# An attention block with a mixture of experts on one core: rows of a round fetched by an indirect DMA in place of gather products

## The reference

```python
router_logits = x @ gate_w                                   # x normed, 256 x 512; 64 experts
routing_weights, selected = jax.lax.top_k(router_logits, 8)
routing_weights = jax.nn.softmax(routing_weights, axis=-1)
...
gate = jax.lax.ragged_dot(hidden_sorted, gate_proj_w, group_sizes)    # 512 -> 192 of each token's experts
up = jax.lax.ragged_dot(hidden_sorted, up_proj_w, group_sizes)
down = jax.lax.ragged_dot(jax.nn.silu(gate) * up, down_proj_w, group_sizes)   # 192 -> 512
...
out = jnp.sum(out * routing_weights[..., None], axis=1)
```

## Time and profile before

| what | us |
|---|---|
| median of 3 runs (lowest, highest) | 346.9 (346.42, 350.45) |
| the profiled execution | 346.79 |
| its span, first to last instruction | 345.1 |

### The profile page before, as it was taken

The page is one execution under the profiler, slowest core; times in us unless marked ns, Lnnn a source line. Parts: engine busy times, 40 slices in busy tenths (PEclk is TensorE's granted clock), DMA queues, the critical chain, the costliest instruction groups (busy, mean ns, idle before and its releaser), DMA issues.

```text
span 345.1 us, 8928 instructions
## 1 busy us (share of the span) xinstructions
PE 319.0 (92%) x3096; PEld 179.7 (52%) x3097; DVE 169.4 (49%) x505; ACT 86.4 (25%) x169; POOL 50.9 (15%) x113
## 2 busy tenths in 40 slices
PE   0599999998999978999999999999999999999994
...
PEclk9999999998599999999999999999999999999998
...
GB/s 66 309 394 392 390 355 228 324 1 3 0 2 2 0 0 163 384 4 295 397 392 392 170 0 315 397 379 162 395 391 178 368 393 392 391 391 391 382 17 62
DMA packets 39755, 83.38 MB, mean 242 GB/s; under 512 B 4648, under 2 KB 12976, under 8 KB 39600
## 3 DMA queue, kind: packets, MB, share of 16 engines
...
q10 hardware_dynamic: 416, 0.04, 0.1%
...
## 4 chain that ended last, share of the span: by engine, by line
PE 80%; DVE 9%; ACT 4%; issue 3%; POOL 1%; DVEq 1%; POOLq 0%; ACTq 0%
PE psum L1219 17%; PE psum L1244 15%; PE psum L1181 12%; PE psum L1156 8%; PE psum L974 4%; PE psum L1013 4%; PE psum L986 4%; PE psum L1228 2%; PE psum L1074 2%; PE psum L1232 2%; PE psum L1104 2%; PE psum L965 2%; ACT store L870 1%; PE psum L1058 1%; PE psum L1128 1%
## 5 line engine op out<-in xcount | busy, mean ns | idle before, releaser
L1219 PE MATMUL psum<-store 128*32 128x384 f32 x896 | 77.4, 486 | 0.7 <-ACT store L912 0.7
L1244 PE MATMUL psum<-store 128*32 128x256 f32 (+1 forms) x672 | 54.0, 454 | 0.0
L1181 PEld LDWEIGHTS psum<-store 128*128 128x128 bf16 x696 | 39.5, 97 | 19.7 <-DVE store L771 11.3
L1219 PEld LDWEIGHTS psum<-store 128*32 128x32 f32 x896 | 28.9, 110 | 37.7 <-issue 32.3
L1181 PE MATMUL psum<-store 128*128 128x128 bf16 x696 | 44.5, 219 | 0.9 <-DVE store L771 0.3
L543 POOL TENSOR_TENSOR store<-store 128x256 f32<-128x256 bf16 x28 | 17.2, 613 | 152.7 <-PE psum L1228 152.2
L933 ACT ACTIVATE y_parts<-psum,w_slot 128x512 fp32r<-128x512 f32 x28 | 19.2, 687 | 74.6 <-PE psum L1244 74.6
L1244 PEld LDWEIGHTS psum<-store 128*32 128x32 f32 x672 | 19.0, 109 | 31.7 <-issue 26.9
L1156 PE MATMUL psum<-y_parts,place_T 128*128 128x512 f32 x116 | 34.3, 416 | 0.9 <-ACT y_parts L933 0.9
L799 DVE TENSOR_SCALAR place_T<-psum 128x256 fp32r<-128x256 f32 x28 | 11.9, 424 | 47.0 <-PE psum L1244 47.0
L912 ACT ACTIVATE store<-psum 128x512 f32<-128x512 f32 x29 | 17.3, 598 | 33.8 <-PE psum L1181 33.8
...
## 6 DMA issues: line engine op xcount, KB each, us to landing
store<-n_L_ffn_gate_proj_w_dram SPq DMA_DIRECT2D x64, 384.0 KB, 6.7
store<-in_L_ffn_up_proj_w_dram SPq DMA_DIRECT2D x64, 384.0 KB, 7.0
store<-n_L_ffn_down_proj_w_dram SPq DMA_DIRECT2D x64, 256.0 KB, 7.2
...
```

Of the source, the lines that this page charges most:

```text
L1181: last = pe.matmul(bank[3][:, c * P:(c + 1) * P], xparts[:, h, part, c, :], chosen_slots[:, h], start=(k == 0), stop=(k == 3 * TH - 1))
L1219: last = pe.matmul(bank[0][quarter, 0:2 * INTER], xs[:, c, quarter], w[:, :, c, :], start=(c == 0), stop=(c == DC - 1))
L1244: last = pe.matmul(bank[6][quarter, cols], hidT[:, k, quarter], ring[r][:, e, at:at + cols.stop - cols.start], start=(k == 0), stop=(k == 2))
```

## The change

The normed x is also stored to DRAM (`x_dram`) by SP. For each round PE multiplies the 0/1 matrix with the token numbers (`tok_b`): a column of row numbers, which DVE writes as integers (`row_no`). POOL starts an indirect DMA with them, which fetches 128 rows of 2 KB into one of two landing buffers; that is done in round v for round v + 3. ACT copies the landed rows of the next round to `x_rows` (the wait for the landing goes through a small POOL instruction, s_land), PE transposes them in four f32 transposes between the first and the second down product, and ACT copies these to xs as before. The picks of four rounds are kept in a ring (`picks`). `mix_t` and its transposes are replaced by a product of the pick with the identity, and one with the team's routing weights, split into three bf16 parts (`w_parts`, by POOL once, ahead of its loop). mix now stands behind the row numbers and ahead of the transposes of the hidden values. POOL counts teams and rounds in registers of its own (`next_round`) and runs in pairs of rounds. The tables in team order are made ahead of the loop. Team 0 has at least two rounds. Round 0 is written out on PE: it makes the row numbers of rounds 2 and 3. Small further edits: a floor of -1e25 for the running maximum and a least value of 1e-30 in a sum of the cross attention.

The core of the diff (declarations, presets and semaphores left out):

```diff
+        total = sb("total", [1, 1], I32)
+        x_dram = nc.dram_tensor("x_normed_rows", (TOK, D), F32)
...
-        turned = carve([P, 2, TH, EXP_N])
+        turned = carve([P, 2, TH, EXP_N + SPILL * TEAM])
         flipped = carve([P, 2, TH, P])
-        pick_t = carve([P, TH, TEAM, BLK], BF16)
-        pick_0 = carve([P, TH, TEAM, BLK], BF16)
+        picks = carve([P, PICKS * TOK], BF16)
...
+        landing = rest.rearrange("p h c q -> p (h c q)")
+        x_rows = store[:, RING * TEAM_W:RING * TEAM_W + D]
...
                 load_team(range(r * TEAM, (r + 1) * TEAM), r)
             sp.wait_ge(s_x1, 2)
             load_team(range((EARLY - 1) * TEAM, EARLY * TEAM), EARLY - 1)
+            for h in range(TH):
+                sp.wait_ge(s_xn, 2 * TH + h + 1)
+                sp.dma_start(x_dram[h * P:(h + 1) * P, :], xn[:, h]).then_inc(s_xd, 16)
             sp.wait_ge(s_op, 2)
             sp.wait_ge(s_cnt, 2)
             load_team(team_of(word_of(EARLY)), EARLY)
...
 
+            ch.step(pool.memset(turned[:, :, :, EXP_N:], 0.0))
+
+            def fetch(u, b):
+                pool.tensor_tensor(ready[:, b:b + 1], zero[:, :], zero[:, :], ALU.subtract).then_inc(s_rdy, 1)
+                pool.indirect_dma_start(landing[:, b * D:(b + 1) * D], None, x_dram[:, :],
+                                        bass.IndirectOffsetOnAxis(ap=row_no[:, b:b + 1], axis=0)).then_inc(s_gat[b], 16)
+
+            pool.wait_ge(s_xp, 2)
+            pool.wait_ge(s_xd, 32)
+            pool.wait_ge(s_idx, 1)
+            fetch(1, 1)
...
             pool.wait_ge(s_tables, 11)
-            pool.wait_ge(s_rk, 1)
-            pool.wait_ge(s_rw, 1)
             pool.wait_ge(s_cnt, 1)
...
-
-            def rounds_of(q, table):
+            team, part = pool.alloc_register("pool_team"), pool.alloc_register("pool_part")
+            pool.reg_mov(team, 0)
+            pool.reg_mov(part, 1)
+            wrap = pool.alloc_register("pool_wrap")
+
+            def next_round():
+                q, r = pool.snap(team, min_val=0, max_val=TEAMS + SPILL - 1), pool.snap(part, min_val=0, max_val=TOK // BLK - 1)
                 count = pool.value_load(rounds[0:1, bass.ds(q, 1)], min_val=1, max_val=TOK // BLK)
...
-                rounds_of(q, rw_rank)
+                pool.reg_mov(wrap, (r + (TOK // BLK + 1) - count) >> 3)
+                w = pool.snap(wrap, min_val=0, max_val=1)
+                pool.reg_add(team, team, w)
+                pool.reg_mov(part, (r + 1) & (7 - w * 7))
+
+            def differences(u):
+                q = pool.snap(team, min_val=0, max_val=TEAMS + SPILL - 1)
+                r = pool.snap(part, min_val=0, max_val=TOK // BLK - 1)
+                pool.wait_ge(s_pk, u)
+                ranks = turned[:, 1, :, bass.ds(q * TEAM, TEAM)]
+                pool.tensor_tensor(apart, ranks.unsqueeze(3).to_broadcast([P, TH, TEAM, BLK]),
+                                   slot_no[:, bass.ds(r, 1), :].unsqueeze(1).to_broadcast([P, TH, TEAM, BLK]),
+                                   ALU.subtract).then_inc(s_ap, 1)
+
+            next_round()
             pool.wait_ge(s_tn, 1)
-            with pool.Fori(EARLY, TEAMS) as q:
-                rounds_of(q, turned)
-
-            pool.wait_ge(s_pk, pool.snap(step) + 1)
-            pool.tensor_tensor(apart, apart, apart, ALU.subtract).then_inc(s_ap, 1)
+            differences(2)
+            next_round()
+            differences(3)
+
+            part1 = w_rest
+            zeros = zero[:, :].unsqueeze(2).to_broadcast([P, TH, EXP_N])
+            weights = turned[:, 0, :, 0:EXP_N]
+            ch.step(pool.tensor_tensor(w_parts[:, :, 0], weights, zeros, ALU.subtract))
+            ch.step(pool.tensor_tensor(part1, weights, w_parts[:, :, 0], ALU.subtract))
+            ch.step(pool.tensor_tensor(w_parts[:, :, 1], part1, zeros, ALU.subtract))
+            pool.tensor_tensor(w_parts[:, :, 2], part1, w_parts[:, :, 1], ALU.subtract).then_inc(s_wp, 1)
+
+            n = pool.value_load(total[0:1, 0:1], min_val=TEAMS + 1, max_val=TEAMS * TOK // BLK)
+            pairs = pool.alloc_register("pool_pairs")
+            pool.reg_mov(pairs, (n + 1) >> 1)
+            with pool.Fori(0, pool.snap(pairs, min_val=1, max_val=TEAMS * TOK // BLK)) as i:
+                for b in range(2):
+                    u = i * 2 + (2 + b)
+                    pool.wait_ge(s_idx, u)
+                    pool.wait_ge(s_row, u)
+                    fetch(u, b)
+                    pool.wait_ge(s_gat[1 - b], i * 16 + 16)
+                    pool.tensor_tensor(ready[:, 2 + b:3 + b], zero[:, :], zero[:, :], ALU.subtract).then_inc(s_land, 1)
+                    next_round()
+                    differences(u + 2)
+            pool.wait_ge(s_gat[1], pool.snap(pairs) * 16 + 16)
+            pool.tensor_tensor(ready[:, 2:3], zero[:, :], zero[:, :], ALU.subtract).then_inc(s_land, 1)
...
-                              slot_no[:, 0:1, :].unsqueeze(1).to_broadcast([P, TH, TEAM, BLK]), ALU.is_equal).then_inc(s_pk0, 1)
+            def pick_of(slot):
+                return picks[:, slot * TOK:(slot + 1) * TOK].rearrange("p (h e s) -> p h e s", h=TH, e=TEAM)
+
+            for u in range(2):
+                dve.tensor_tensor(pick_of(u), rank[:, :, 0:TEAM].unsqueeze(3).to_broadcast([P, TH, TEAM, BLK]),
+                                  slot_no[:, u:u + 1, :].unsqueeze(1).to_broadcast([P, TH, TEAM, BLK]), ALU.is_equal).then_inc(s_pk, 1)
...
+            def write_pick(slot, u):
+                dve.wait_ge(s_ap, u - 1)
+                dve.tensor_scalar(picks[:, bass.ds(slot * TOK, TOK)], apart.rearrange("p h e s -> p (h e s)"), 0.0, None,
+                                  ALU.is_equal).then_inc(s_pk, 1)
+
+            def write_rows(column, u):
+                dve.wait_ge(s_idp, u)
+                dve.tensor_copy(row_no[:, bass.ds(column, 1)], bank[7][:, 0:1]).then_inc(s_idx, 1)
+
+            write_rows(1, 1)
             dve.wait_ge(s_cnt, 1)
-            dve.wait_ge(s_ap, 1)
-            write_pick()
+            write_pick(2, 2)
+            write_pick(3, 3)
+            write_rows(0, 2)
...
-                    dve.wait_ge(s_ap, v + 2)
-                    dve.wait_ge(s_xg, v + 1)
-                    dve.wait_ge(s_mx, v + 1)
-                    write_pick()
                     dve.wait_ge(s_si, v + 1)
                     dve.tensor_tensor(hid[:, 0:MAIN_I], silu[:, 0:MAIN_I], bank[0][:, INTER:INTER + MAIN_I], ALU.mult)
                     dve.tensor_tensor(hid_twice, silu[:, MAIN_I:].unsqueeze(2).to_broadcast([P, TAIL_I, 2]),
@@ -793,10 +866,15 @@
                     for half in range(2):
                         last = dve.tensor_scalar(hidT[:, 1 + half], bank[1][:, P:2 * P], side[:, half:half + 1], None, ALU.mult)
                     last.then_inc(s_htt, 1)
-                    dve.wait_ge(s_mtp, v + 2)
-                    dve.tensor_reduce(w_slot[:, :], bank[2][:, 0:TOK], AX.X, ALU.add).then_inc(s_ws, 1)
-                    dve.wait_ge(s_y, v + 1)
+                    dve.wait_ge(s_land, v + 1)
+                    write_rows((v + 1) & 1, v + 3)
+                    dve.wait_ge(s_mtp, v + 1)
+                    lc = Chain(dve, s_dvw, base=v)
+                    lc.step(dve.tensor_tensor(w_lanes, bank[2][:, TOK:TOK + 3 * TEAM].rearrange("p (n e) -> p n e", n=3),
+                                              lane[:, :].unsqueeze(1).to_broadcast([P, 3, TEAM]), ALU.mult))
+                    dve.tensor_reduce(w_slot[:, :], w_lanes.rearrange("p n e -> p (n e)"), AX.X, ALU.add).then_inc(s_ws, 1)
                     dve.tensor_scalar(place_T[:, :], bank[2][:, 0:TOK], 0.0, None, ALU.not_equal).then_inc(s_mt, 1)
+                    write_pick(v & (PICKS - 1), v + 4)
                     dve.wait_ge(s_yh, v + 1)
                     dve.scalar_tensor_tensor(y_parts[:, 1], bank[6], w_slot[:, :], y_parts[:, 0], ALU.mult, ALU.subtract).then_inc(s_yl, 1)
                     dve.reg_add(step, step, 1)
...
             act.wait_ge(s_xg, 1)
             copy_gathered()
+            act.wait_ge(s_tnp, 1)
+            act.activation(turned[:, :, :, 0:EXP_N], bank[6][:, 0:4 * EXP_N].rearrange("p (a h e) -> p a h e", a=2, h=TH), ACT.Copy).then_inc(s_tn, 1)
             act.wait_ge(s_cnt, 1)
...
                     act.wait_ge(s_gu, v + 1)
                     act.activation(silu, bank[0][:, 0:INTER], ACT.Silu).then_inc(s_si, 1)
+                    act.wait_ge(s_land, v + 1)
+                    act.activation(x_rows, landing[:, bass.ds(((v + 1) & 1) * D, D)], ACT.Copy).then_inc(s_row, 1)
                     act.wait_ge(s_xg, v + 2)
                     copy_gathered()
...
-            pe.wait_ge(s_pk0, 1)
-            gather(pick_0)
+            pe.wait_ge(s_pk, 1)
+            gather(picks)
+
+            def row_numbers(slot):
+                for h in range(TH):
+                    last = pe.matmul(bank[7][:, 0:1], picks[:, bass.ds(slot * TOK + h * P, P)], tok_b[:, h:h + 1],
```

(60 more changed lines are left out.)

132 lines of the change are left out of this document (53 added, 79 removed).

## The result

The changed kernel took 353.4 us (median of 4 runs, 352.11 to 355.83), the kernel before 346.66 us beside it: a ratio of 1.0225, interval 1.0166 to 1.0283. It is slower, by about 2%. The forecast was 349.3 us with a range of 339 to 360. The profiled execution took 352.11 us with a span of 350.4; all that follows is counted in it, against the 345.1 of the earlier trace rows.

The account below looks back on a forecast made before the run. PE bounds each round, the weights come second: rounds of 7.16 us, 4.0 us lost in round 0, round 27 at 334.1 after weights and fetches, then 13.6 less 0.1: span 347.6, time 349.3 us, range 339 to 360.

Parts of the forecast that it names:

- A round, 7.16 us: One expert round on PE, gate/up to gate/up: 7.16 us against 7.28 before, bounds 6.5 and 7.6.
- the stall and the switches of the forecast: PE around the down products: a stall of some 0.37 us, and 0.31 us for switching between quarters and full array.
- Round 0, 4.0 us lost: First round, POOL doing all in line: 11.1 us instead of 7.16, 4.0 us lost, bounds 1 and 8.
- POOL's fetch, issue 1.3, landing 4.4 us: POOL's indirect DMA in each round: 1.3 us to issue (upper end 5), 4.4 us to land (between 2.2 and 6.7).
- Rival B: Slower: POOL's fetch sets the round; with an issue of 6 us a round is 8.1 us, time 370; chance 0.18.
- Weights end at 334.1, a wait of 4.4 us: Before round 27: PE stands 4.4 us for weights, and the round starts at 334.1 instead of 331.51.
- 62.8: Weight queues: time in us of the five loads behind team 7, taken as measured from 265.22 to 328.0.
- 6.0: Weight queues: time in us that nine fetches at 0.67 add to the five loads behind team 7.
- D, the fetches cost nothing: Weight queues: the fetches cost the weights nothing, round 27 starts at 329.7 and the time is 344.9 us; chance 0.12.
- C, the clock: Last round: the wait before round 27 drops PE's clock, about 5 us more, 354.3 us; chance 0.15.
- A, faster: PE's rounds: the stalls don't come, order overlaps better; 6.5 us a round, time 338.4 us; chance 0.17.

Follow-up runs that it names:

- ahead: The changed kernel with PE's four transposes of x_rows moved from between the down products to ahead of them: 346.43 us, ratio 1.0025 to the kernel before.
- no_fetch: The changed kernel without the indirect DMAs in the loop and the waits for them (tokens not right): 344.83 us, ratio 0.9826 to the kernel before.
- thin: The changed kernel with fetched rows of 64 B in place of 2 KB (tokens not right): 348.93 us, ratio 1.0108 to the kernel before.
- bytes_in_before: The kernel before, plus a plain POOL DMA of 128 rows of 2 KB that nobody reads, 29 in all: 353.81 us, ratio 1.0218.
- kept_warm: The changed kernel with 24 idle PE products before the wait for the last team's weights: 352.09 us, ratio 1.0152 to the kernel before.

## Why the prediction was right

The mechanism came as forecast, and the time, 2.8 us over the forecast in the profiled execution and 4.1 in the median, lies well inside the range. The range is wide, though: of the change itself the forecast had 2.4 us (346.9 to 349.3), and 6.7 were measured. Step by step:

- **A round, 7.16 us: right.** 7.12 measured, and for the reasons given: a stall before the down products (0.23 us instead of 0.37), the run of transposes and the second half of down as laid out, and the copy of xs on the edge (it did reach PE's load, by 0.17 us). ahead shows that the stall and the split of the down products were worth 0.53 us a round, close to the stall and the switches of the forecast together (0.37 + 0.31 = 0.68).
- **Round 0, 4.0 us lost: right.** 10.88 us for 7.12, 3.8 lost. POOL's list came a little faster than worked out: second fetch issued by 140.16 (141.1), the landing told at 140.19 (141.2), round 1 at 142.85 (143.5), from a start 0.4 us earlier than forecast.
- **POOL's fetch, issue 1.3, landing 4.4 us: near enough to change nothing.** 0.97 and a median of 6.3 us. Rival B needed an issue of 5.0 or a landing over some 7 us. The median landing came within 0.7 us of that second condition; POOL's wait for a landing (L612) shows once in 28 times (3.3 us, in round 1, and that round is 7.12 us long all the same).
- **Weights end at 334.1, a wait of 4.4 us: right in kind, mis-sized.** The wait is there, with a DMA as releaser, but 7.2 us, and round 27 starts at 335.58. Round 18 started 1.4 us earlier than forecast (263.92 for 265.3), and the stretch behind it took 71.7 us where the sum had 62.8 + 6.0 = 68.8. The term that failed is the 62.8. It ended the loads at 328.0, the edge of the window of the earlier trace rows, while 265, 110 and 10 GB/s still flowed in the three microseconds around it; no_fetch shows what the five loads take with these rounds, 66.7 us up to the start of the products. The fetches were over-sized, if anything: 5.0 us by the difference of those two runs, not 6.0. By the queue's share each took 0.79 us, which is then not all at the weights' cost. The 5.0 is not a clean price either: the changed kernel's queues still had 0.3 MB of team 10's load at the start of this stretch (23.91 MB of weights in it, where five teams are 23.6) and ran on without a pause, while those of no_fetch stood empty there. That the time came within 3 us owes something to luck: an early start (1.4 us) and an over-sized price of the fetches (1.0) took off most of what the 62.8 lacked (3.9).
- **D, the fetches cost nothing: refuted** by thin, no_fetch and bytes_in_before.
- **C, the clock: its condition came, its price did not.** It had 0.15 and a price of 5 us, from "most of the 6.8 us" at half clock. The clock fell during the wait, while nothing ran, and was back between 338 and 340: only gate/up was slow, 4.25 us instead of 2.76. 1.5 us by kept_warm. The chance was too low: the earlier trace rows had a fall behind 2 us with PE busy for 1.18 of them, and the forecast's own wait was 4.4 us with nothing at all. The Trainium skill ("TensorE: Matmul & The Clock Gate", Why this matters for your kernels) warned of long gaps between bursts; the trace agrees, 0.50 behind 5.9 us of idling.
- **A, faster: half of it true, in another kernel.** Rounds of 6.5 us are there with the transposes moved (6.59), but the time was 346.4, not A's 338.4. In ahead team 3 ended at 205.24 and not at 201.4 (round 0 took 12.06 us), round 27 began 125.2 us behind that and not 122.4, and E was 14.5 us with a gate/up of 4.48, not 12.9: 3.8 + 2.8 + 1.6 us.

From 349.3 to the profiled 352.1 it is thus 1.5 us of later weights and 1.3 us at the end (the clock, 1.5, less small things). The medians lie another 1.3 us apart because the runs do: the four of the changed kernel reach from 352.11 to 355.83.

At 1.0225, with an interval from 1.0166 to 1.0283, the result stands on the edge between "within 2%" and "slower by over 2%".

Left open: why the five loads take 66.7 us in no_fetch, when the kernel before started the same loads 1.5 us later (265.61 for 264.14) and had them at nearly the same time. The early start is lost at once: from 264 to 273 both moved the same, 2.14 and 2.13 MB. It is not for want of places, since SP does not wait for PE once in no_fetch between 264.2 and the end of the loads; its queues ran at 181 to 278 GB/s in most of the microseconds from 265 to 272, with DMAs started and not yet landed. Why they were that slow no run shows.
